# First pass of a five-engine kernel: GpSimd takes eight of every 64 convolution rows, partial sums move to PSUM, and the loop body covers four images

## What is computed

```python
x = jax.lax.conv_general_dilated(sx, w_down, window_strides=(2, 2), padding=((1, 1), (1, 1)),
                                 feature_group_count=c2, dimension_numbers=('NCHW', 'OIHW', 'NCHW'))
...
# labels of the channels, a mixture fit, a gate for each channel, bilinear up, + sx
# second layer, on x2 = that result:
P = P_CONST                                  # (128*128, 64), 64 low cosine frequencies
xP = jnp.einsum('bcn,nk->bck', x2, P)
...
```

## Time and profile before

| | us |
|---|---|
| median of 3 runs | 3707.73 (3704.37 to 3709.26) |
| the profiled execution | 3707.28 |
| its span, first to last instruction | 3705.5 |
| busy over the span: PE | 3104.3 (84%) |
| busy over the span: DVE | 2962.2 (80%) |
| busy over the span: ACT | 1873.8 (51%) |
| busy over the span: POOL | 637.1 (17%) |

### The profile page before, as it was taken

One profiled execution on the slowest core, in us unless ns is written; L12 is line 12 of the kernel. 1 busy time (PEld: TensorE's weight loads), 2 busy tenths in 40 slices (PEclk: granted clock), 3 DMA queues, 4 the chain that ended last, 5 costly groups with the idle time before them and its releaser, 6 DMA issues. The chain is left out here.

```text
span 3705.5 us, 65837 instructions
## 1 busy us (share of the span) xinstructions
PE 3104.3 (84%) x23258; PEld 2248.5 (61%) x23258; DVE 2962.2 (80%) x3430; ACT 1873.8 (51%) x4307; POOL 637.1 (17%) x325
## 2 busy tenths in 40 slices
PE   7999989999899949994557888988788898888777
PEld 3454545454454526642326777878777787878776
DVE  5999999999999971204446978989898888979877
ACT  4555555555455524231214565565656556565654
POOL 0000000000000000000002333333333333333333
PEclk9999999999999979596668999999999999999999
DMA  6655665566556623440033889888888988888997
GB/s 268 257 235 209 245 260 227 209 255 257 219 215 259 258 107 130 182 183 22 0 127 136 333 332 342 335 323 331 331 329 335 340 335 323 337 328 333 344 339 298
DMA packets 190940, 947.58 MB, mean 256 GB/s; under 512 B 13505, under 2 KB 13633, under 8 KB 170626
## 3 DMA queue, kind: packets, MB, share of 16 engines
q1 hardware_dynamic: 181378, 909.48, 63.5%
q0 software_dynamic: 9216, 33.56, 2.2%
HBM read 638.90 MB, written 301.99 MB: 254 GB/s over the span
## 5 line engine op out<-in xcount | busy, mean ns | idle before, releaser
L190 DVE SCALAR_TENSOR_TENSOR first_acc<-first_x,first_wd,first_acc 128x1024 f32<-128x1024 f32 (+1 forms) x1088 | 1297.8, 1273 | 57.3 <-ACT first_acc L215 45.9
L1260 PE MATMUL second_o<-second_right,second_left 128*128 128x128 f32 x8192 | 1097.9, 284 | 177.1 <-POOL second_left L1044 99.3
L1260 PEld LDWEIGHTS second_o<-second_right,second_left 128*128 128x128 f32 x8192 | 1014.3, 198 | 230.6 <-issue 216.6
L1504 DVE SCALAR_TENSOR_TENSOR second_x<-second_o,second_shift,second_x 128x512 f32<-128x512 f32 x1024 | 733.4, 738 | 231.8 <-PE second_o L1260 230.5
L1044 POOL TENSOR_TENSOR second_left<-second_mid_copy,second_coef_rep 64x1024 f32<-64x1024 f32 x256 | 602.4, 2353 | 1731.2 <-ACT second_mid_copy L1367 1725.7
L219 ACT ACTIVATE first_xT<-first_tp 128x512 f32<-128x512 f32 x1024 | 608.5, 597 | 533.3 <-PE first_tp L245 532.7
L245 PE MATMUL first_tp<-all_const,first_x 128*128 128x128 f32 x4096 | 678.8, 291 | 81.4 <-issue 43.7
L245 PEld LDWEIGHTS first_tp<-all_const,first_x 128*128 128x128 f32 x4096 | 441.3, 143 | 462.1 <-issue 446.1
L257 PE MATMUL first_freq<-first_xT,first_p 128*64 128x256 f32 x4096 | 666.0, 406 | 17.4 <-ACT first_xT L219 7.8
L1346 ACT ACTIVATE second_mid<-second_dd,all_inter 128x128 f32<-128x128 f32 x1024 | 327.1, 390 | 387.2 <-DVE second_mid L1485 384.0
L257 PEld LDWEIGHTS first_freq<-first_xT,first_p 128*64 128x64 f32 x4096 | 210.4, 135 | 193.3 <-issue 178.9
(11 more groups left out here) (222 smaller groups left out, 1976.8 us busy)
## 6 DMA issues: line engine op xcount, KB each, us to landing
second_x<-in_x SPq DMA_DIRECT2D x256, 1024.0 KB, 10.2
out<-second_x SPq DMA_DIRECT2D x256, 1024.0 KB, 6.5
first_x<-in_x SPq DMA_DIRECT2D x48, 4224.0 KB, 25.3
first_x<-in_x SPq DMA_DIRECT2D x16, 4096.0 KB, 15.0
gather_d<-downsampled SPq DMA_DIRECT2D x24, 2048.0 KB, 12.3
downsampled<-first_acc POOLq DMA_DIRECT2D x64, 512.0 KB, 11.7
second_dd<-downsampled SPq DMA_DIRECT2D x64, 512.0 KB, 11.0
first_p<-in_p_cols SPq DMA_DIRECT2D x1, 4096.0 KB
```

The source lines that it names most:

```text
L190: nc.vector.scalar_tensor_tensor(out=acc[c][:, :, left:], in0=tap_window(xt[c], (s, dh, dw), OUT1), scalar=wd[:, t, k:k + 1], in1=acc[c][: ...
L1260: last = nc.tensor.matmul(ob[n][:, r, :], left[a][:, r, n, :], right[a][:, r, :], start=True, stop=True)
L1504: nc.vector.scalar_tensor_tensor(out=xt[i][:, n // S, n % S, rows, :], in0=ob[n][:, :, :], scalar=shift[:, n:n + 1], in1=xt[i][:, n // S, ...
```

## The change

It has six parts, all in the first pass.

1. GpSimd does the 17 taps of the last eight output rows of chunk 3 in each image, each as two instructions: a tensor_scalar (window times weight, into product) and a tensor_tensor (acc plus product, into acc). Its code is written out for all 16 images.
2. VectorE does chunks 0 and 1 as before, 34 instructions of 16 rows. Then it does chunk 2 in two halves and the upper half of chunk 3, 51 instructions of 8 rows. The sums of its taps 2 to 17 lie in PSUM (partial0 and partial1); the last tap writes acc in SBUF. Its order of the taps changes too.
3. To free the PSUM banks, TensorE's transposes get two banks instead of four, and the fold writes into the unused part of the frequency banks.
4. ScalarE's first tap of chunk 3 moves from ahead of quad 48's copy to ahead of quad 34's.
5. The stores move from GpSimd's queue to SP's, each ahead of the load of the same chunk. Chunk 3's store waits for both VectorE and GpSimd.
6. The loops of VectorE, ScalarE and TensorE run twice instead of eight times, with four batch elements (eight images) written out in the body.

```diff
-TAPS = [(s, dh, dw) for dw in (0, 1) for dh in (-1, 0, 1) for s in range(S)] + \
-       [(s, dh, -1) for dh in (-1, 0, 1) for s in range(S)]
+TAPS = [(s, dh, dw) for dw in (0, -1, 1) for dh in (-1, 0, 1) for s in range(S)]
...
+TP_BANKS = 2
+UNROLL1 = 4
+POOL_CHUNK = 3
+FIRST_TAPS = [0, QUADS, 2 * QUADS, 2 * QUADS + 2]
+STEPS = [TAPS_LEFT, TAPS_LEFT, 2 * TAPS_LEFT, 2 * TAPS_LEFT]
...
-        tp = [sc.ps(f"tp{i}", [P, 4, P]) for i in range(SLOTS)]
+        tp = [sc.ps(f"tp{i}", [P, 4, P]) for i in range(TP_BANKS)]
         freq_ps = [sc.ps(f"freq{t}", [P, 512]) for t in range(T)]
-        sum_ps = sc.ps("sum", [P, 512])
+        sum_ps = [bank[:, S * P:S * P + S * UV] for bank in freq_ps]
+        product = sc.sb("product", [P, OUT1 // 2, WD])
+        partial = [sc.ps(f"partial{i}", [P, OUT1, WD]) for i in range(2)]
...
+                def store(i, c):
+                    sp.wait_ge(tapped[c], i * STEPS[c] + STEPS[c] + FREE)
+                    if c == POOL_CHUNK:
+                        sp.wait_ge(upper_tapped, i * TAPS_LEFT + TAPS_LEFT + FREE)
+                    sp.dma_start(xd.rearrange("b t g n -> (b t) g n")[i, :, c * OUT1 * WD:(c + 1) * OUT1 * WD],
+                                 acc[c][:, :, :].rearrange("g h w -> g (h w)")).then_inc(stored[c], 16)
...
+                with sp.Fori(0, B * T - 1) as i:
+                    for c in range(CH1):
+                        store(i, c)
+                        load(i + 1, c)
...
+                for i in range(B * T):                          # GpSimd
+                    pool.wait_ge(x_in[c], i * 16 + 16)
+                    pool.wait_ge(started, i * CH1 + c + 1)
+                    for n, (s, dh, dw) in enumerate(TAPS[1:]):
+                        if n > 0 or i > 0:
+                            pool.wait_ge(tapped[c], done + 2 * n)
+                        nc.gpsimd.tensor_scalar(product[:, :, left:],
+                                                tap_window(xt[c], (s, dh, dw), OUT1 // 2, OUT1 // 2),
+                                                wd[:, i % T, weight_of(s, dh, dw)], None, ALU.mult
+                                                ).then_inc(tapped[c], 1)
+                        pool.wait_ge(tapped[c], done + 2 * n + 1)
+                        nc.gpsimd.tensor_tensor(acc[c][:, rows, left:], acc[c][:, rows, left:], product[:, :, left:],
+                                                ALU.add).then_inc(tapped[c], 1)
...
+                def tap(t, c, n, rows, mine):                   # VectorE
+                    before = acc[c] if n == 0 else mine
+                    after = acc[c] if n == TAPS_LEFT - 1 else mine
...
-                with act.Fori(0, B) as b:
-                    for t in range(T):
-                        i = b * T + t
+                with act.Fori(0, B // UNROLL1) as r:
+                    for n_image in range(UNROLL1 * T):
+                        t, i = n_image % T, r * UNROLL1 * T + n_image
                         for q in range(quads):
-                            slot, c = q % SLOTS, q // QUADS
-                            if q % QUADS == 0:
+                            slot = q % SLOTS
+                            if q in FIRST_TAPS:
+                                c = FIRST_TAPS.index(q)
```

More of the change, by code:

```diff
@@ L123, in first_pass @@
         started = sc.sem("started")
-        tapped = [sc.sem(f"tapped{c}") for c in range(2)]
-        chunk_free = [sc.sem(f"chunk_free{c}") for c in range(CH1)]
-        xd_out = [sc.sem(f"xd_out{i}") for i in range(CH1)]
+        tapped = [sc.sem(f"tapped{c}") for c in range(CH1)]
+        upper_tapped = sc.sem("upper_tapped")
         stored = [sc.sem(f"stored{i}") for i in range(CH1)]
@@ L153, in _ @@
                         sp.dma_start(p_sb[:, :, :], p_cols.rearrange("w (h k) -> w h k", k=UV)).then_inc(p_in, 16)
-                with sp.Fori(1, B * T) as i:
-                    for c in range(CH1):
-                        load(i, c)
+                def store(i, c):
[4 more added lines that the diff above has]
+                                 acc[c][:, :, :].rearrange("g h w -> g (h w)")).then_inc(stored[c], 16)
+                start_free(sp, stored)
+                with sp.Fori(0, B * T - 1) as i:
+                    for c in range(CH1):
+                        store(i, c)
+                        load(i + 1, c)
+                for c in range(CH1):
+                    store(B * T - 1, c)
+                for c in range(CH1):
+                    sp.wait_ge(stored[c], B * T * 16 + FREE)
             @block.gpsimd
@@ new lines, in _ @@
+                start_free(dve, [*tapped[:3], upper_tapped])
+                def tap(t, c, n, rows, mine):
+                    s, dh, dw = TAPS[1 + n]
+                    left = 1 if dw < 0 else 0
+                    row0, count = rows.start, rows.stop - rows.start
+                    before = acc[c] if n == 0 else mine
+                    after = acc[c] if n == TAPS_LEFT - 1 else mine
+                    return nc.vector.scalar_tensor_tensor(
+                        out=after[:, rows, left:], in0=tap_window(xt[c], (s, dh, dw), count, row0),
+                        scalar=wd[:, t, weight_of(s, dh, dw)], in1=before[:, rows, left:],
+                        op0=ALU.mult, op1=ALU.add)
@@ new lines, in _ @@
+                with dve.Fori(0, B // UNROLL1) as r:
+                    for n_image in range(UNROLL1 * T):
+                        t, i = n_image % T, r * UNROLL1 * T + n_image
+                        for n in range(TAPS_LEFT):
+                            for c in (0, 1):
+                                if n == 0:
+                                    dve.wait_ge(x_in[c], i * 16 + 16)
+                                    dve.wait_ge(started, i * CH1 + c + 1)
+                                    if c == 0:
+                                        dve.wait_ge(tapped[2], i * STEPS[2] + FREE)
+                                    else:
+                                        dve.wait_ge(upper_tapped, i * TAPS_LEFT + FREE)
+                                else:
+                                    dve.wait_ge(tapped[c], i * STEPS[c] + n + FREE)
+                                tap(t, c, n, slice(0, OUT1), partial[c]).then_inc(tapped[c], 1)
+                        c, half = 2, OUT1 // 2
+                        for n in range(TAPS_LEFT):
+                            for h in range(2):
+                                if n == 0 and h == 0:
+                                    dve.wait_ge(x_in[c], i * 16 + 16)
+                                    dve.wait_ge(started, i * CH1 + c + 1)
+                                    dve.wait_ge(tapped[0], i * STEPS[0] + STEPS[0] + FREE)
+                                elif n > 0:
+                                    dve.wait_ge(tapped[c], i * STEPS[c] + 2 * n + h - 1 + FREE)
+                                tap(t, c, n, slice(h * half, (h + 1) * half), partial[0]).then_inc(tapped[c], 1)
+                            if n == 0:
+                                dve.wait_ge(x_in[POOL_CHUNK], i * 16 + 16)
+                                dve.wait_ge(started, i * CH1 + POOL_CHUNK + 1)
+                                dve.wait_ge(tapped[1], i * STEPS[1] + STEPS[1] + FREE)
+                            else:
+                                dve.wait_ge(upper_tapped, i * TAPS_LEFT + n + FREE)
+                            tap(t, POOL_CHUNK, n, slice(0, half), partial[1]).then_inc(upper_tapped, 1)
@@ L232, in _ @@
                 pe.wait_ge(top_zero, 1)
-                with pe.Fori(0, B) as b:
-                    for t in range(T):
-                        i = b * T + t
+                with pe.Fori(0, B // UNROLL1) as r:
+                    for n_image in range(UNROLL1 * T):
+                        t, i = n_image % T, r * UNROLL1 * T + n_image
                         def transpose(q):
```

54 lines of the change are left out of this document (17 added, 37 removed).

## The result

| | median, us | ratio to before |
|---|---|---|
| before, 4 runs beside the changed kernel | 3706.05 (3701.45 to 3709.26) | |
| after, 4 runs | 3663.32 (3656.68 to 3665.35) | 0.9883 [0.9865, 0.9900] |

A forecast was written before the change was run, and what follows sets the result against it. VectorE bounds the first pass at 81.9 us per image; afterwards a two-image chain would, at 79.5. Saving 34.2 us there and 7 us at its end, 41 off 3707.3, gave 3666 us, range 3628 to 3715 (likeliest case 3650 to 3690).

The forecast's parts named there:

- VectorE's image: VectorE's work per image in the first pass: 73.9 us of taps plus 1.8 us for meeting GpSimd, 75.7 us.
- the rival built on it: PSUM operands cost VectorE time, up to 57 ns per tap or 4.8 us per image: about 3703 us; chance 0.15.
- The two-image chain: VectorE's image, chunk 3's store and load, then TensorE to the next chunk-1 tap: 158.2 us per two images.
- TensorE alone: Rival: TensorE alone bounds the first pass at 77.3 us per image, 3633 us; chance 0.24.
- The clock: TensorE's half clock after a wait of about 3 us: 1.7 us, every other stop, so 0.4 us per image.
- The turn: The one loop turn left, on the chain: 6.2 us stop plus 1.7 us for the clock, 8 us.
- The end: VectorE's work in the first pass ends at 1320.9 us against 1355.1; the tail up to the next pass saves 7 us.
- the term that was mis-sized: GpSimd's work per image: 17 pairs of 1.18 us twice plus 0.1 us hand-over, 42 us.
- my own threshold: GpSimd's chain, work + 26.4 + 1.6 us, equals 79.5 us per image at 51.5 us of work, 3.0 us per pair.
- the load's 26.4 us: Chunk 3's store and load: 25.3 us to landing behind chunk 2's, plus 1.1 us for two issues.
- Two of my signs: Right: GpSimd pairs under 2.6 us, done before VectorE's phase ends. GpSimd rival: SP waits for GpSimd before chunk 3's store.
- The rival's 3820 us: GpSimd becomes the bound; at 61.7 us of work, 89.7 us per image and near 3820 us; chance 0.12.

The follow-up runs named there:

- Tap 40: The changed kernel with ScalarE's first tap of chunk 3 at quad 40 in place of 34: 3647.96 us, ratio 0.9842.
- the kernels with 13 taps: The changed kernel with GpSimd leaving out the last 4 of its 17 taps: 3661.40 us with chunk 3's first tap at quad 34, 3635.97 us at quad 40.
- one body: The changed kernel with chunk 3's first tap at quad 40 and all 16 images in one loop body: 3631.54 us, ratio 0.9803.
- before with the long body: The kernel before with only its loop bodies written out for four batch elements: 3712.08 us, ratio 1.0011.
- sums in SBUF: The changed kernel with VectorE's partial sums in SBUF (acc) again, everything else the same: 4100.13 us, ratio 1.1056.

## Why the prediction was right

**VectorE's image.** Predicted 73.9 us of taps with PSUM for nothing. The spacings are 1.185 and 0.655 us where I had 1.191 and 0.655. So writing PSUM costs nothing that shows here either, and the rival built on it is out. The three first taps that meet GpSimd cost less than the 1.8 us I gave them: 402.42 to 405.39 is 2.97 us for three, 1.0 over three plain ones. The image from its second tap on takes 73.6 us (363.29 to 436.85), 74.8 with the first, against 75.7.

**The two-image chain.** This was the step that decided, and it held in its parts: counted from VectorE's second tap, 363.29, to its last 73.7 us (75.7 less a tap of 1.2 predicted), to the load's landing 27.2 (26.4), and from there to the end of the next image's tap of chunk 1 at 522.4, 58.2 (56.1 and that 1.2). The sum is 159.1, and 159.2 lie between the two taps; I had 158.2, and 0.8 for the clock. One link is other than I had it: the landing, 27.2 us after VectorE's last tap, hangs on chunk 2's issue at 436.99 and not on chunk 3's, which comes out the same here because the two are 1.4 us apart. Tap 40 confirmed it by taking it away. TensorE alone, my second case, is what that kernel shows: 77.5 us per image with 77.3 predicted. Its end came later than I had it, VectorE's at 1299.1 against 1287.9, with three images at 79.0 us, and GpSimd's 6.2 us behind that, and the time is 3648 us where I had 3633.

**The clock.** The half clock after a late load cost 1.5 us (1.7 taken), and it came after four of the eight waits, as supposed.

**The turn.** I charged 8 us. In after it is 6.3: the two images across it took 686.21 - 521.17 = 165.0 us between ScalarE's taps, where the other pairs took 157.2 to 159.5 (158.7 on the mean). The 8.6 us show only where TensorE alone is the bound.

**The end.** VectorE's end: 1320.9 predicted, 1316.4 measured: 1.7 us by the turn, some 2.3 by 15 images of 79.35 in place of 79.5 us, the rest at the start. The tail gave 5.5 us and not 7. Half of the tail is now GpSimd, which ends 3.2 us after VectorE; I had it done earlier.

**GpSimd, the term that was mis-sized.** "17 x 2.46 = 42 us" was 52.5 to 54.9: 1.64 for the tensor_scalar (I had 1.18, half of the nearest two-input row), 1.29 for the tensor_tensor, 0.1 between. The length supposition failed for one operation by 39% and for the other by 9%. By my own threshold ("equal to 79.5 at 51.5 us") GpSimd should then have been the bound, at about 81 us per image. It wasn't, because the threshold took the load's 26.4 us as fixed. That number holds for a load issued right behind another of the same size. Issued 11 us later it lands in 15.3. A chain through GpSimd therefore has some 10 us more room than I gave it. Two of my signs misled by the same mistake: GpSimd's pairs were not under 2.6 us (they are 3.1 us apart) and not done before VectorE, and SP did wait for GpSimd, 31.7 us in eight times, and still GpSimd was not the bound. The prediction came out right because the threshold's error covered the term's error: two mistakes, which tap 40 and the kernels with 13 taps took apart. The rival's 3820 us for 61.7 us of work would have been too high for the same reason: with 15.3 us for the landing its chain reaches 79.5 us per image only at 79.5 - 15.3 - 1.1 - 1.6 = 61.5 us of work (an estimate); that size was not run.

## What to carry to other kernels

- A landing time read from a trace holds for the queue's state at that moment. Before it goes into a chain as a constant, ask what was in flight ahead of it, and what happens if the producer is late.
- Look for the chain that closes only after two rounds of a loop. Here a tap written at quad 34 cost 15 us against quad 40 and 11 us against quad 48, where it stood before, though no engine was full. What the earlier start gives GpSimd counts only at the end of the pass. Quad 40 leaves room to both the load and GpSimd.
- When the code behind the change is the same, measure at the place where the changed part ends. That showed steps of 6 us which the times of four or five runs did not.
- A mean over instructions of one form can hide a few that are many times as long. Here the mean was 4.4 us, the median 2.0 and the longest 54. Look at all three before building on one.

## What was not expected of the hardware

- GpSimd's tensor_scalar with one input of 128x512 takes longer (1.61 us median) than its tensor_tensor with two (1.28 us median), and its step of two is worth only 0.05 us. What makes it slow stays open.
- TensorE's clock also fell to half behind idle times of only 0.47 and 1.19 us at the start of an image, in three of the images with the tap at 40, and not in the others with the same or nearly the same two gaps. TensorE's timeline of one without and one with:

```profile
264.80 0.66 PE L311 MATMUL first_tp<-all_const,first_x 128*128 128x128 f32 x4 [1.17 <-ACT first_xT L284]
...
497.48 1.10 PE L311 MATMUL first_tp<-all_const,first_x 128*128 128x128 f32 x4 [1.19 <-ACT first_xT L284]
```

  What tells such images apart was not found. With one body the gap is 1.09 us in place of 1.19, and it happened in one image.
- A turn of the loop stops TensorE for 5 to 6 us on the mean of each kernel. VectorE stopped for 6.7 us at the one turn of before with the long body.
- A GpSimd instruction of 1.6 us can last over 50 us beside an unbroken row of VectorE instructions with two SBUF inputs (sums in SBUF, eight times).
- Of two 4.2 MB loads issued up to 11 us apart, the second lands 26 to 28 us after the first's issue, whenever its own was.
